# A transformer, mamba and expert kernel: the order of every engine's instructions, once sorted by model times, written out letter by letter

## The reference, cut to what matters

```python
x = L0_attn_x_in                                    # (4, 1024, 256)
x = x + ln(encoder(ln(x)))     # 4 layers: ln, q k v, linear attention over all tokens, Wo, ln, relu(h @ W1) @ W2
x = x + ln(lora_mix(ln(x)))    # base product plus 8 gated low-rank adapters
x = x + ln(mamba(ln(x)))       # in-projection, 4-tap conv, softplus rates, scan with 16 states, out-projection
x = x + ln(experts(ln(x)))     # argmax of 8 experts, at most 320 tokens for each, relu(h @ w1) @ w2
```

## Time and profile before

| what | us |
|---|---|
| median of 3 runs | 2798.64 (2791.62 to 2802.93) |
| profiled execution, span | 2801.1 |
| PE busy | 2391.1 (85%) |
| DVE busy | 1810.1 (65%) |
| POOL busy | 1723.6 (62%) |
| ACT busy | 1618.4 (58%) |
| 4 layers of batch 0 | 0 to 463 |
| layers of batches 1, 2, 3 | 463 to 1026, to 1627, to 2207 |
| units 6 and 7 | 2207 to 2607 |
| experts | 2607 to 2801 |

### The profile page before, as it was taken

How to read it: one execution, slowest core, us unless ns; L and a number is a source line. 1 busy time by engine, 2 the same in 40 slices (tenths; PEclk the granted TensorE clock), 3 DMA queues, 4 the chain that set the end, 5 groups by cost and what they waited for, 6 DMA issues and landing times. The chain is left out here.

```text
span 2801.1 us, 40293 instructions
## 1 busy us (share of the span) xinstructions
PE 2391.1 (85%) x13172; PEld 1965.7 (70%) x13172; DVE 1810.1 (65%) x3883; ACT 1618.4 (58%) x3649; POOL 1723.6 (62%) x1988
## 2 busy tenths in 40 slices
PE   6999998899989858798989887989898766666898
PEld 5889987687869755686878756877788532122698
DVE  4232334678677774887378667784777766879566
ACT  4555666677656654666476655766666556523153
POOL 1111214298659873898369847985598755778356
PEclk8999999999979988899999998999999878778899
DMA  4435233223413232232223133232221232323142
GB/s 159 170 139 192 95 116 135 92 63 104 120 63 95 69 120 88 72 112 66 100 65 113 50 132 100 77 114 74 78 91 46 72 119 73 81 81 88 47 146 93
DMA packets 123899, 273.85 MB, mean 98 GB/s; under 512 B 9213, under 2 KB 64125, under 8 KB 114092
## 3 DMA queue, kind: packets, MB, share of 16 engines
q1 hardware_dynamic: 120108, 263.37, 29.4%
q0 software_dynamic: 3584, 7.92, 0.8%
HBM read 215.93 MB, written 58.48 MB: 98 GB/s over the span
## 5 line engine op out<-in xcount | busy, mean ns | idle before, releaser
L1991 POOL TENSOR_TENSOR sb_sc<-sb_bc,sb_du 128x512 f32<-128x512 f32 x512 | 660.8, 1296 | 107.6 <-issue 38.3
L2004 POOL TENSOR_TENSOR sb_ya<-sb_ya,sb_sc 128x512 f32<-128x512 f32 x384 | 494.8, 1289 | 27.3 <-DVE sb_sc L1245 27.1
L680 PE MATMUL ps<-sb_w,sb_fa 128*128 128x256 f32 x2048 | 494.2, 385 | 5.2 <-ACT sb_fa L1601 5.2
L468 PE MATMUL ps<-sb_hT,sb_w 128*128 128x256 f32 x2048 | 405.2, 297 | 15.7 <-issue 5.9
L680 PEld LDWEIGHTS ps<-sb_w,sb_fa 128*128 128x128 f32 x2048 | 376.6, 193 | 49.8 <-ACT sb_fa L1601 3.9
L1736 ACT ACTIVATE ps<-sb_dl,sb_aneg 128x512 f32<-128x512 f32 x512 | 349.9, 687 | 99.3 <-DVE sb_sc L1245 91.0
L1233 DVE TENSOR_TENSOR_SCAN ps<-ps,sb_sc 128x512 f32<-128x512 f32 x240 | 292.9, 1224 | 101.5 <-ACT ps L1736 94.1
L468 PEld LDWEIGHTS ps<-sb_hT,sb_w 128*128 128x128 f32 x2048 | 329.2, 193 | 34.5 <-issue 23.2
L1233 DVE TENSOR_TENSOR_SCAN ps<-ps,sb_hl,sb_sc 128x512 f32<-128x512 f32 x240 | 306.8, 1283 | 67.2 <-ACT ps L1736 63.2
L1245 DVE TENSOR_TENSOR sb_sc<-ps,sb_bc 128x512 f32<-128x512 f32 x480 | 321.8, 671 | 0.0
L1601 ACT ACTIVATE sb_fa<-ps,sb_b1n 128x256 f32<-128x256 f32 x512 | 209.8, 464 | 147.3 <-PE ps L468 146.9
(11 more groups left out here) (262 smaller groups left out, 5055.1 us busy)
## 6 DMA issues: line engine op xcount, KB each, us to landing
sb_bc<-b_and_c SPq DMA_DIRECT2D x128, 512.0 KB, 5.0
sb_w<-w_parts SPq DMA_DIRECT2D x15, 2048.0 KB, 7.7
sb_wq<-w_qkv_parts SPq DMA_DIRECT2D x15, 1536.0 KB
sb_w<-in_w SPq DMA_DIRECT2D x16, 1024.0 KB
sb_raw<-in_mw SPq DMA_DIRECT2D x16, 1024.0 KB, 9.7
gate_z<-sb_xin SPq DMA_DIRECT2D x30, 256.0 KB, 2.2
sb_zt<-gate_z SPq DMA_DIRECT2D x30, 256.0 KB, 3.8
expert_in<-sb_bb SPq DMA_DIRECT2D x5, 1032.0 KB, 12.9
```

Source lines behind the costliest of these rows:

```text
L468: ins = pe.matmul(bank, lhs[x], rhs[y], start=(first and m == 0), stop=(last and m == 2), skip_group_check=True)
L680: ins = pe.matmul(acc[:, v * D:(v + 1) * D], fa[i % 3][:, h * 256 + v * 128:h * 256 + (v + 1) * 128], w2[:, 2 * f + h, :], start=(f == 0 a ...
L1991: p.tensor_tensor(db[m % RING], bc[:, i % 3, 0, :], dus[u][:, c, :], ALU.mult).then_inc(S("bm"), 1)
L2004: p.tensor_tensor(yas[u][:, c, :], yas[u][:, c, :], db[m % RING], ALU.add).then_inc(S("ad"), 1)
```

## The change

All model times and the functions that work them out are deleted. Every `yield` is bare, and `weave` takes a string for each engine: each letter names the stream whose next piece is written next. The strings have 1600 letters for PE, 1462 for DVE, 1853 for ACT, 1336 for POOL and 393 for SP, as many of each letter as there were pieces. The pieces themselves, their waits, and their instructions are untouched; which PSUM bank of the ring a piece gets follows from the order.

```diff
-LAYER = 104.0
-ENC = (5.71, 458.78, 1126.31, 1807.18)
...
-UNIT = (510.45, 829.39, 1168.77, 1527.12, 1852.95, 2208.16, 2544.61, 2691.41)
...
+PE_TURNS = (
+    "aaabbeedeefbfdfefebdffaeedaffgggghggggihhhiiicacajjjkkkjcjkjjkkkjcjjkjkkjkbakeedjjakkjjbkkeefbfdbefeffedfedffg"
...
-def weave(*streams):
-
-    heads = [[next(s), n, s] for n, s in enumerate(streams)]
-    while heads:
-        head = min(heads, key=lambda h: (h[0], h[1]))
-        try:
-            head[0] = next(head[2])
-        except StopIteration:
-            heads.remove(head)
+def weave(turns, *streams):
+    for stream in streams:
+        next(stream)
+    for letter in turns:
+        next(streams[LETTERS.index(letter)], None)
...
                     for t in range(2):
-                        yield keys_at(b, l, g, t)
+                        yield
                         bank, freed = ring.take()
...
-                        yield rates_at(u) + RATE_AT[u][0] + 1.5 * c
+                        yield
                         bank, freed = ring.take()
...
                 for h, b, g in later:
-                    yield ahead_at(h, 3)
+                    yield
                     e.wait_ge(S("nn"), 2 * h + 1)
```

More of the change, by code:

```diff
@@ L1364, in experts_ahead @@
             def experts_ahead():
-                yield ahead(30.0)
+                yield
                 low_second(0)
-            weave(weights(), *[inputs(g) for g in range(4)], inputs_ahead(), experts_ahead(),
-                  low_parts("tr1", lambda b, l, g: lay(b, l, BASE_A[kind(b, l)][g] + TR_DVE)),
-                  low_parts("tr3", lambda b, l, g: lay(b, l, BASE_F[kind(b, l)][g] + TR_DVE)), queries(), keys(), key_products(),
+            weave(DVE_TURNS, weights(), *[inputs(g) for g in range(4)], inputs_ahead(), experts_ahead(),
+                  low_parts("tr1"),
+                  low_parts("tr3"), queries(), keys(), key_products(),
                   attended(), projected(), fed(), *[group_tails(g) for g in range(4)], unit_input(), rates(), unit_steps(), unit_output())
@@ L1783, in experts_ahead @@
             def experts_ahead():
-                yield ahead(15.0)
+                yield
                 high_first(0)
-                yield ahead(25.0)
+                yield
                 high_second(0)
-                yield RATES[1] + 12.0
+                yield
                 high_first(1)
-            weave(weights(), first_norms(), inputs_ahead(), squares1(), squares2(), experts_ahead(),
-                  layer_norms(ln1, norm1_at), layer_norms(ln2, norm2_at),
-                  high_parts("tr1", lambda b, l, g: lay(b, l, BASE_A[kind(b, l)][g] + TR_ACT)),
-                  high_parts("tr3", lambda b, l, g: lay(b, l, BASE_F[kind(b, l)][g] + TR_ACT)), queries(), keys(), attended(), feed(),
+            weave(ACT_TURNS, weights(), first_norms(), inputs_ahead(), squares1(), squares2(), experts_ahead(),
+                  layer_norms(ln1), layer_norms(ln2),
+                  high_parts("tr1"),
+                  high_parts("tr3"), queries(), keys(), attended(), feed(),
                   *[group_tails(g) for g in range(4)], unit_input(), rates(), unit_steps(), unit_output())
@@ L2058, in experts_ahead @@
                 for n in range(2):
-                    yield RATES[1] + 16.0 if n else ahead(20.0)
+                    yield
                     low_first(n)
-            weave(constants_made(), first_norms(), inputs_ahead(), layer_norms(ln1, norm1_at), layer_norms(ln2, norm2_at), *[group_tails(g) for g in range(4)],
+            weave(POOL_TURNS, constants_made(), first_norms(), inputs_ahead(), layer_norms(ln1), layer_norms(ln2), *[group_tails(g) for g in range(4)],
                   experts_ahead(), unit_input(), softplus(), inputs_times_b(), sums_of_states(), late_products(), unit_output())
@@ L2367, in sp_program @@
             q.wait_ge(S("d_wb"), 64)
-        def after(b, l, off, first):
-            if b == 0 and l == 0:
-                return first
-            pb, pl = (b, l - 1) if l else (b - 1, L - 1)
-            return lay(pb, pl, off)
         pe_program(nc.tensor)
```

511 lines of the change are left out of this document (242 added, 269 removed).

## The result

The changed kernel takes 2580.55 us (median of 4 runs, 2580.28 to 2589.14), the one before 2797.12 on the same chip: a ratio of 0.9235, 95% interval 0.9216 to 0.9254. That is 216.6 us less. I had forecast 45 and a range whose fast end was 2695. It is the slowest of its four executions, 8.6 us over their median, as the profiled one of before was the slowest of its own.

The account below looks back on a forecast made before the run. PE bounds the kernel, busy 2391.1 of 2801.1 us, with 225 us idle in layers of batches 1 to 3. Terms -39 - 14 + 0 + 0 + 8 = -45 gave a 2756 us span, 2753.5 median; range 2695 to 2812.

Parts of the forecast that it names:

- the rival called "more": Order takes nearly half of PE's 225 us idle in layers of batches 1 to 3: -107, 2692 us; chance 15%.
- Only idle time can change: Premise for the gains: nothing removed or added, no instruction changes its price; only idle time can change.
- Inside the layers: Layers outside boundary windows, 147 us PE idle: small moves of both signs, 0 us, bounds -49 and +20.
- The odd units' rates: Odd units starting about 25 to 60 us earlier: layers, not units, bound these stages; 0 on PE.
- Inner boundaries: Windows between batches: next batch's keys ahead of waiting tails fill half of PE's 78 us idle, -39 us.
- Final boundary: Last layer to unit 6's first scan, 2207 to 2293: half of PE's 28.4 us idle goes, -14 us.
- Units 6 and 7: Units after the layers, no layers beside them: DVE called busiest, 309 of 400 us; no term given.
- Layer 0: Batch 0's first layer: later batches' input norms moved into its first 160 us crowd ACT, +8 us (0 to 16).
- the slower rival: Layer 0's inputs_ahead chain stalls in-order queues; each us above 19.9 a round costs 6, 2818.5 us; chance 18%.
- The lock's price: Odd units' rate products on DVE beside busy POOL, sharing a port: 1.20 for 0.69 us; 0 on path, bound +12.

## Why the prediction was wrong, step by step

**The view was right, the weight was wrong.** That idle time of PE in the layers of batches 1 to 3 was the thing to look at held: 117 of 225 us went. This is the rival called "more" (nearly half), to which I gave 15%. Its sum was added up wrong: 112 + 14 - 8 is 118 and not 107, which gives 2681 for 2692. Even so it was 100 us too high, since all my terms were idle time.

**"Only idle time can change": failed.** I wrote that no instruction changes its price. PE's busy time fell by 66.7 us in these stages and by 74.3 over the kernel, for the same 13172 records. The granted clock was 0.952 in place of 0.921, and no term of the sum stood for it.

**Inside the layers: the step that failed most.** I wrote 0, with a bound of -49. The traces give 120 us outside the boundary windows. I had reasoned that hundreds of small moves carry both signs. The layers show two places instead. The last layers of the batches (7, 11, 15) are 22, 18 and 22 us shorter, 62 in all, and there it is the tails: put back, they cost 33, 12 and 19 us. Groups 0 to 2 have their tails inside the batch's last layer, ahead of the boundary windows that I had drawn. The pairs in which the odd unit takes over are 21, 17 and 18 us shorter, 56 in all, and the odd units' rates, put back, cost 13, 11 and 11 of them. The first layers behind their windows give the last 1 or 2 us. I had also read the earlier trace rows too simply: of its 81.3 us only 48 stood at tails, and 33 were the layers' own, which I then priced at nothing.

**The odd units' rates: failed.** I held that units don't bound these stages, and priced the earlier start at 0. Put back alone they cost 36 us. The gap from even to odd unit did become 28, 49 and 50 us, and PE was 90 to 100% busy in it, in place of 78 to 92%.

**Inner boundaries: mechanism right, size low.** 63.6 us for 39, and the wait of 20.4 us went with nothing in its place. My 39 were idle time, and of idle time 45.6 us went; the other 18 are the busy time that I had held fixed. **Final boundary: right.** 18 us for 14.

**Units 6 and 7: no term at all.** 24 us came from a stretch that I passed over as DVE's; together with the final boundary its order is worth 48 by the run with the old order there.

**Layer 0: right in sign, 22 us at its end for 8, 13.6 over batch 0.** The norms account for 10.5 of the 22, near my 8, but not for the loss over batch 0: put back, they leave it as long. I had written that what they free in layers 1 to 3 is worth nothing, and it was worth 9.8 us. The rest of the 22 is mostly work: 40 more matmul records stand in layer 0, which I had not counted. Five other kernels with the old order there end layer 0 some 4 us earlier than the profiled execution of before, so this figure is good to a few us only. The chain of the slower rival did run at a rate near the critical one (the third pass of the 24 pieces on ACT spans 39.7 to 173.9 us, eleven groups or 5.5 rounds, 24.4 us a round, for 19.9 that I had called free), but what it delays is made good in layers 1 to 3. The weights of layer 1, for which PE might have waited, cost it nothing: layer 1 took 96.5 us in place of 106.7.

**The lock's price: not there to pay.** The product of the earlier trace rows, which I expected at 1.20 us, took 0.68 to 0.69 in 10 of the 12 places in units 1, 3 and 5 of the changed kernel, and 1.10 and 1.16 in the other two. DVE's busy time is 8.3 us more over the kernel, inside the bound of 12, but that agreement is luck: this product is not its cause.

**What stays open.** Tails 99, rates 36 and late stages 48 make 183 of 216, and the first two add. They are prices of taking a part out of a finished order by my merge, which may itself block queues (the merges into the old order all made it slower), so they don't measure the parts well. That the parts would gain as much when put into the old order is not shown: no run put the tails there behind the next batch's keys with the rest as it was. Layer 6, which went from 140.9 to 105.0, gives back only 4.8 with the rates and 1.1 with the tails. With layer 5, which grew by 14.5, the pair is 21.4 us shorter and gives back 12.8 with the rates, so some 9 us there, 5 in layers 9 and 10 and 7 in layers 13 and 14, have no cause that I can name. That PE's matmuls were shorter by 74 us over the kernel goes with the clock; whether the clock was worth time by itself stays open: fill at waits brought none, and nothing else was tried.

## What to carry to other kernels

When a written order replaces a modelled one on all queues, price the idle time of the bounding engine over the whole stage by what its waits have in common (here one tile in 19 waits), not by the one place where the cause can be read off; that a stream isn't the bound by its length does not make its place free. The order of one engine can't be tried alone: among strange orders the new PE string was 15% slower than the old one in its own company. When a piece is put back or put in by its time, look at its neighbours afterwards: the tails "in their new places" still stood ahead of the work that was to go before them. To find where such a gain lies, cut the program in time, with all queues changed at the cut: the layers behind it show their order's own durations at once.

## What the runs showed of the hardware

The same 13172 matmul records took 2316.8 us at a mean granted clock of 0.952, 2391.1 at 0.921, 2425.8 at 0.909 (PE's order old) and 2484.6 at 0.884 (PE's order new alone): 24 to 25 us for each 0.01. Idle matmuls put into waits raised the clock a little and brought no time: from 0.925 to 0.932 in the kernel before (medians of the executions), with 6 us more, and from 0.951 to 0.957 up to 0.956 to 0.960 in the changed one, with 6 us more and overlapping intervals. That does not make the clock worthless: among the ten executions of one filled kernel, 0.936 went with 2784.04 us and 0.926 with 2804.27. Which of the two leads isn't shown.

Idle fp32 matmuls of 128x128 (two records each) were 184 records in 20.71 us back to back, 0.11 us a record, while a single record lasts 0.28.
